# FP4 MLP of a two-layer block: rounding put one pair later, the residual added by TensorE, its result copied by ScalarE

## The reference

```
def fp4_quant_dequant(x):             # blocks of 16 along the last dimension
    scale = maximum(max(abs(xb)) / 6, 1e-12)
    q = GRID[searchsorted(MID, abs(xb / scale))] * sign(xb) * scale
def fp4_linear(x, w):                 # both rounded, then x @ w.T
gate = fp4_linear(x, w_gate)          # 128 -> 352
y = fp4_linear(x, w_up)               # 128 -> 352
h = silu(gate) * y
x = x + tanh(g_ffn[1]) * fp4_linear(h, w_down)     # 352 -> 128
```

## Time and profile before

| | |
|---|---|
| median of 3 runs | 299.23 us (297.94 to 299.8) |
| the profiled execution | 295.81 us |
| its span | 293.8 us |
| mean granted TensorE clock | 0.971 |
| busy: PE / PEld / DVE / ACT / POOL | 89% / 69% / 68% / 55% / 41% |

### The profile page before, as it was taken

The page is one execution under the profiler, slowest core; times in us unless marked ns, Lnnn a source line. Parts: engine busy times, 40 slices in busy tenths (PEclk is TensorE's granted clock), DMA queues, the critical chain, the costliest instruction groups (busy, mean ns, idle before and its releaser), DMA issues.

```text
span 293.8 us, 6298 instructions
## 1 busy us (share of the span) xinstructions
PE 261.2 (89%) x2190; PEld 203.5 (69%) x2190; DVE 199.5 (68%) x538; ACT 161.4 (55%) x368; POOL 120.8 (41%) x172
## 2 busy tenths in 40 slices
PE   8999899999899999999999998987857869696955
PEld 5655466666578789999999975554645547374855
DVE  3997588889987744322222269746287999998981
ACT  2579975555786666666666647224443824443421
POOL 4573879995203042299522015302253131313121
PEclk9999999999999999999999999999998969797999
DMA  7997000000001197767777300000000000000001
GB/s 204 370 363 316 3 2 0 2 2 2 2 3 20 73 379 325 294 287 288 288 289 300 134 0 2 1 3 0 0 0 0 2 1 0 18 19 19 18 19 56
DMA packets 12159, 30.15 MB, mean 103 GB/s; under 512 B 992, under 2 KB 5216, under 8 KB 12000
## 3 DMA queue, kind: packets, MB, share of 16 engines
q1 hardware_dynamic: 12128, 29.75, 26.8%
HBM read 9.75 MB, written 1.05 MB: 37 GB/s over the span
## 4 chain that ended last, share of the span: by engine, by line
PE 63%; DVE 17%; ACT 7%; issue 5%; POOL 3%; DMA 2%; SPq 1%; DVEq 0%; ACTq 0%; POOLq 0%
PE ps L1307 11%; PE ps L1296 11%; PE ps L1156 5%; PE ps L1130 4%; PE ps L1485 4%; PE ps L1143 4%; DVE s_region L279 4%; PE ps L1058 3%; PE ps L1424 3%; PE ps L1049 2%; DVE s_small L228 2%; PE ps L1166 2%; PE ps L1050 2%; DVE s_region L995 2%; DVE s_small L1005 1%
## 5 line engine op out<-in xcount | busy, mean ns | idle before, releaser
L573 ACT ACTIVATE s_region<-ps,s_region 128x128 f32<-128x128 f32 x144 | 41.1, 369 | 22.0 <-PE ps L1296 21.8
L868 DVE SCALAR_TENSOR_TENSOR s_ctxT<-ps,s_region,s_ctxT 128x64 f32 x72 | 18.1, 282 | 44.3 <-PE ps L1307 44.2
L1296 PE MATMUL ps<-s_region 128*128 128x128 f32 x288 | 38.5, 276 | 0.3
L1307 PE MATMUL ps<-s_region 128*128 128x128 f32 x288 | 37.9, 275 | 0.0
L286 POOL TENSOR_TENSOR s_region<-s_region,s_small 128x704 f32<-128x704 f32 (+2 forms) x13 | 17.5, 1343 | 46.5 <-DVE s_region L279 46.5
L1296 PEld LDWEIGHTS ps<-s_region 128*128 128x128 f32 x288 | 35.0, 192 | 1.0 <-DMA s_region<-s_wall 0.6
L1307 PEld LDWEIGHTS ps<-s_region 128*128 128x128 f32 x288 | 35.0, 192 | 0.2 <-issue 0.2
L251 POOL TENSOR_TENSOR s_small<-s_small,s_par 128x4 f32<-128x4 f32 (+3 forms) x14 | 15.5, 1107 | 43.2 <-DVE s_small L234 43.2
L1485 PE MATMUL ps<-s_region 128*128 128x352 f32 x64 | 26.4, 570 | 2.3 <-ACT s_region L650 2.3
L398 POOL COPY s_region<-s_xt 128x64 f32 x72 | 14.8, 238 | 32.1 <-PE ps L1296 22.0
L733 DVE TENSOR_REDUCE s_small<-ps 128x16 f32<-128x1024 f32 x16 | 19.6, 1225 | 9.9 <-PE ps L1130 9.9
(11 more groups left out here) (216 smaller groups left out, 509.0 us busy)
## 6 DMA issues: line engine op xcount, KB each, us to landing
s_region<-s_wall SPq DMA_DIRECT2D x36, 514.0 KB, 3.0
s_wall<-wall SPq DMA_DIRECT2D x8, 514.0 KB, 9.0
s_par<-par SPq DMA_DIRECT2D x1, 1316.0 KB, 10.5
s_x<-x SPq DMA_DIRECT2D x2, 512.0 KB, 6.8
out<-s_x SPq DMA_DIRECT2D x8, 128.0 KB, 1.8
s_region<-ffn SPq DMA_DIRECT2D x1, 560.0 KB, 3.6
s_ctxT<-ctxT SPq DMA_DIRECT2D x2, 256.0 KB, 4.2
s_ctxT<-ctxT SPq DMA_DIRECT2D x1, 512.0 KB, 6.7
```

The source lines that it names most:

```text
L573: ins = act.activation(hg[j % 3][:, c, :], ps[:, j % 3, RPT * S * c:RPT * S * (c + 1)], ACT.Gelu, bias=wbuf[j % 6][:, FF + FC * D + c:FF + ...
L1296: ins = mm(ps[:, j % 3, RPT * S * c:RPT * S * (c + 1)], w[:, P * c:P * c + P], xg[j % 4], start=True, stop=True)
L1307: ins = mm(ps[:, 4 + j % 2, 0:RPT * S], w[:, FF + D * c:FF + D * c + D], hg[j % 3][:, c, :], start=(c == 0), stop=(c == FC - 1))
```

## The change

VectorE's `pair_step(q)` does product, maximum, scale, reciprocal and shrinking of pair q first, and then the rounding of q-1. Its `finish` is gone. The gate is multiplied into the turned w_down by ScalarE as it copies it. In `down(q)` TensorE first multiplies x of the pair (256 columns) with the identity into bank 7 and then adds the six products to it; ScalarE's new `finish(q)` copies the sum back to x. On TensorE down now stands ahead of gate_up in an iteration and works on pair q-3, turn_h on q-2, and turn_x stands ahead of keep_clock. On ScalarE the copy to hT is of pair q-2, behind finish(q-3).

```diff
@@ weights_turned
-                act.copy(dst, ps[:, 2 + g % 2, 0:MT * P]).then_inc(m["wq_used"], 1)
+                src = ps[:, 2 + g % 2, 0:MT * P]
+                ins = act.activation(dst, src, ACT.Identity, scale=tg[:, 3:4]) if g == 2 else act.copy(dst, src)
+                ins.then_inc(m["wq_used"], 1)
@@ scalar
+            def finish(q):
+                act.wait_ge(m["dn_done"], q + 1)
+                act.copy(x[:, 2 * q:2 * q + 2, :].rearrange("p t d -> p (t d)"), ps[:, 7, 0:2 * D]).then_inc(m["x4_done"], 1)
+
+            for q in range(PAIRS + 2):
                 if q + 1 < PAIRS:
                     silu(q + 1)
                 if q < PAIRS:
                     magnitude(q)
                 if q in (1, 3):
                     x_magnitude((q + 3) // 2)
-                if q >= 1:
-                    act.wait_ge(m["ht_done"], q)
-                    act.copy(hT[(q - 1) % 2]...).then_inc(m["ht_used"], 1)
+                if q >= 3:
+                    finish(q - 3)
+                if q >= 2:
+                    act.wait_ge(m["ht_done"], q - 1)
+                    act.copy(hT[q % 2]...).then_inc(m["ht_used"], 1)
                 if q in (0, 2, 4):
                     turned_x(q // 2 + 1)
+            finish(PAIRS - 1)
@@ vector, pair_step(q)
                     dve.tensor_tensor(hh[u], sg[u], ps[:, 3:5, 0:MLP], ALU.mult).then_inc(m["hh_done"], 1)
-                if second:
-                    dve.wait_ge(m["hm_done"], q)
-                    dd.step(fp4_off(dve, hd[w], hm[w], hh[w]...))
-                    fp4_off(dve, hd[w], hm[w], hd[w]).then_inc(m["hd_done"], 1)
...
-                if q >= 3:
-                    finish(q - 3)
...
                     fp4_shrunk(dve, blocks(flat), blocks(flat), spread(hin[n3], 2 * NH)).then_inc(m["hv_done"], 1)
+                if 1 <= q <= PAIRS:
+                    dve.wait_ge(m["hm_done"], q)
+                    if q >= 3:
+                        dve.wait_ge(m["hq_done"], q - 2)
+                    dd.step(fp4_off(dve, hd[w], hm[w], hh[w]...))
+                    fp4_off(dve, hd[w], hm[w], hd[w]).then_inc(m["hd_done"], 1)
@@ tensor
+                mm(ps[:, 7, 0:2 * D], ident, x[:, 2 * q:2 * q + 2, :].rearrange("p t d -> p (t d)"), start=True, stop=False)
...
-            for q in range(PAIRS + 2):
+            for q in range(PAIRS + 3):
+                if q >= 3:
+                    down(q - 3)
                 if q + 1 < PAIRS:
                     gate_up(q + 1)
-                if q >= 2:
-                    down(q - 2)
-                if 1 <= q <= PAIRS:
-                    turn_h(q - 1)
+                if 2 <= q <= PAIRS + 1:
+                    turn_h(q - 2)
+                if q in (0, 2, 4):
+                    turn_x(q // 2 + 1)
                 if q < 2:
                     keep_clock(4, 7)
                 if PAIRS - 2 <= q <= PAIRS:
                     keep_clock(9 if q == PAIRS - 2 else 3, 0)
-                if q in (0, 2, 4):
-                    turn_x(q // 2 + 1)
```

More of the change, by code:

```diff
@@ L678, in _ @@
             normalise(act, 12, 16, m["xn_d"], 14)
-            for q in range(PAIRS + 1):
+            def finish(q):
+                act.wait_ge(m["dn_done"], q + 1)
+                act.copy(x[:, 2 * q:2 * q + 2, :].rearrange("p t d -> p (t d)"), ps[:, 7, 0:2 * D]).then_inc(m["x4_done"], 1)
+            for q in range(PAIRS + 2):
                 if q + 1 < PAIRS:
@@ L685, in _ @@
                     x_magnitude((q + 3) // 2)
-                if q >= 1:
-                    act.wait_ge(m["ht_done"], q)
-                    act.copy(hT[(q - 1) % 2].rearrange("p a k b -> p a (k b)"), ps[:, 5:7, 0:MT * P]).then_inc(m["ht_used"], 1)
+                if q >= 3:
+                    finish(q - 3)
+                if q >= 2:
+                    act.wait_ge(m["ht_done"], q - 1)
+                    act.copy(hT[q % 2].rearrange("p a k b -> p a (k b)"), ps[:, 5:7, 0:MT * P]).then_inc(m["ht_used"], 1)
                 if q in (0, 2, 4):
                     turned_x(q // 2 + 1)
+            finish(PAIRS - 1)
         @block.vector
@@ L990, in pair_step @@
                 u, w, n3 = q % 2, (q - 1) % 2, q % 3
-                first, second = q < PAIRS, 1 <= q <= PAIRS
-                if first:
+                if q < PAIRS:
                     dve.wait_ge(m["sg_done"], q + 1)
@@ L995, in pair_step @@
                     dve.tensor_tensor(hh[u], sg[u], ps[:, 3:5, 0:MLP], ALU.mult).then_inc(m["hh_done"], 1)
-                if second:
-                    dve.wait_ge(m["hm_done"], q)
-                    dd.step(fp4_off(dve, hd[w], hm[w], hh[w].rearrange("p a n -> p (a n)")))
-                    fp4_off(dve, hd[w], hm[w], hd[w]).then_inc(m["hd_done"], 1)
-                if first:
                     if q >= 3:
@@ L1012, in pair_step @@
                     fp4_shrunk(dve, blocks(flat), blocks(flat), spread(hin[n3], 2 * NH)).then_inc(m["hv_done"], 1)
[L1014 to L1017, removed]
+                if 1 <= q <= PAIRS:
+                    dve.wait_ge(m["hm_done"], q)
+                    if q >= 3:
+                        dve.wait_ge(m["hq_done"], q - 2)
+                    dd.step(fp4_off(dve, hd[w], hm[w], hh[w].rearrange("p a n -> p (a n)")))
+                    fp4_off(dve, hd[w], hm[w], hd[w]).then_inc(m["hd_done"], 1)
             def out_and_stats(g):
@@ L1029, in _ @@
             x_scale(1)
-            for q in range(PAIRS + 3):
+            for q in range(PAIRS + 1):
                 pair_step(q)
@@ L1508, in down @@
                         n = min(P, MLP - P * k)
-                        ins = mm(ps[:, 7, D * t:D * t + D], hT[q % 2][0:n, t, k, :], wdT[0:n, k, :], start=(k == 0), stop=(k == MT - 1))
+                        ins = mm(ps[:, 7, D * t:D * t + D], hT[q % 2][0:n, t, k, :], wdT[0:n, k, :],
+                             start=False, stop=(t == 1 and k == MT - 1))
                 ins.then_inc(m["dn_done"], 1)
```

## The result

The kernel after takes 300.32 us (median of 20 runs, 298.88 to 303.65), the kernel before 298.56 (20 runs, 295.34 to 299.94). The ratio is 1.0084, 95% interval 1.0049 to 1.012: slower by 2.5 us, 1.5 to 3.6. The ratio is one of means and leaves out the runs over 1.5% above the fastest of their kernel, so it gives 2.5 us where the medians lie 1.8 us apart. The difference is clear of noise, yet under the 1% that the prediction took as the bound between slower and unchanged. I had said 303.1.

What follows compares the result with a forecast made beforehand. VectorE bounds the kernel before; TensorE, at 5.85 us per pair, was to bound plain steps after. Span 293.8 + 3.9 = 297.7, profiled execution 299.7, and the median's 3.4 shift gave 303.1 us, range 299.8 to 307.

Steps and rivals of the forecast that it cites:

- rival A: The walk's own outcome: TensorE becomes the bound in plain steps; 303.1 us, own range 301.5 to 305, chance 0.43.
- Rival C: Milder: x's roundings don't wait for GpSimd, or the clock stays high over the 5 us gap; 301.1 to 301.9, chance 0.28.
- Part 1: VectorE: plain step 5.06 against 5.43 us; x_scale pays 0.7 and x_round 1.3 each, meeting GpSimd's unscale.
- Part 2: TensorE: copy exposed between turn_h and down, identity product 0.43; 5.85 us per pair, so TensorE bounds plain steps.
- Part 3: ScalarE: gate in the weights costs 0, finish takes 0.45 us, standing ahead of the copy that down(q-2) awaits.
- The walk: Step-by-step timing of the new order from product(1) to the last finish: span ends 3.9 us later, 297.7.
- step 2: TensorE idle 5.1 us before turn_x(2), then slow clock through down(0), 3.9 us; gate_up(4) sets product(4) at 259.85.
- rival B: Clock recovers later, or falls again around turn_x(3), slowing gate_up(5) or gate_up(6) by 1.7 to 2.5; 305 to 307, chance 0.18.
- Rival D: VectorE sets the pace to the end, winning 0.37 in seven steps; -3.0 us, giving 296.2, chance 0.11.

Runs made afterwards that it cites:

- e1: Kernel after with gate_up(q+1) ahead of down(q-3) on TensorE; 1.007 of before, stage 64.66 us.
- e7: Kernel after with x_round and x_scale ahead of the pair's rounding on VectorE, x_unscale ahead of the pair's unscale on GpSimd; 0.9949 of before, stage 59.45 us.
- e11: e7 with keep_clock(3) for keep_clock(9), 10 idle products ahead of turn_x(2), 8 ahead of down(1); 0.9906 of before, median 295.51 us.
- e4: Kernel before with only VectorE's rounding of q-1 moved behind the shrinking of q, finish staying on VectorE; 1.0101 of before, stage 62.88 us.
- e10: Kernel after with 21 idle products ahead of turn_x(2) and 6 ahead of turn_x(3) on TensorE; stage 62.68 us.
- e2: Kernel after with x_round and x_scale ahead of the pair's rounding on VectorE, GpSimd's order unchanged; 1.0109 of before, stage 62.63 us.
- e3: Kernel after with the edits of both e1 and e2; 1.0149 of before, stage 65.35 us.
- e6: Kernel after with keep_clock(3) instead of keep_clock(9) in the iteration of gate_up(7); 1.011 of before, stage 62.53 us.
- e9: Kernel after without the identity product and the gate in the weights, finish back on VectorE; 1.0103 of before, stage 63.21 us.

## Why the prediction was right

Direction and range came out: 300.32 lies just inside 299.8 to 307. The mechanism is that of rival A, but the number is not: A's own range was 301.5 to 305, and 300.32 falls into the 299 to 301 that I had put under C for the case that nothing is seen. The size was too large by 2.8 us, and the side of the 1% bound was the wrong one (I gave slower 0.58, within 0.35).

- **Part 1, VectorE's new order.** Right. Products of a plain step are 5.12 to 5.13 apart where nothing else bounds (e1, e7, e11), for 5.06 in the sum; L1010 is 0.19. x_scale pays 0.69 (0.87 - 0.18), for 0.7. x_round(2) pays 1.07 net (4.21 - 3.14), for 1.3. e4 shows that this part alone is enough for the loss ahead of product(7).
- **Part 2, TensorE's new order.** Right as a bound, 5.95 for 5.85, and the identity product is the 0.43 estimated (255.90 to 256.33 in e10). But e1 shows that covering the copy in the steps wins nothing by itself, since the same work then lies in the tail.
- **Part 3.** Finish 0.37, for 0.45.
- **The walk.** In the first profile, counted from product(0), it gave 12.3 us for product(2), measured 12.34; 28.9 for product(4), measured 27.54; 36.6 for product(5), measured 35.07; 43.0 for product(6), measured 42.90; 49.0 for product(7), measured 48.85; tail 15.6, measured 15.48. The error at product(4) is step 2: I let the slow clock last through all of down(0), 3.9 us, and it took 2.68 with its identity product (257.00 to 259.68). gate_up(4) was done in time, and VectorE set product(4). The agreement at product(6) is luck: the 1.6 us too many at product(5) were met by a fall of the clock at down(2) and gate_up(6) that rival B had and A had not. The repeat fits the walk without it: 28.60 for product(4), which waited for gate_up(4) as the walk has it, then 36.14, 42.32 and 48.26, and a tail of 15.49. In the tail the walk is right for its reason too: four downs are left there, 3.48 to 3.59 us apart (3.5 forecast), where before has three.
- **From the profile to the runs.** This is where the 2.8 us lie. 0.7 of them come from the base: three runs gave 299.23 for before, 20 runs give 298.56. The other 2.1 are the walk's +3.9, which the medians show as 1.8 and the ratio as 2.5. The walk's figure is fair for the stage, which lost 3.1 to 3.7 in the profiles, but the interval of the runs, 1.5 to 3.6, holds the 3.1 and neither 3.7 nor 3.9. Why the runs lose less than the profiled stages is open. Ahead of the stage, product(0) lies at 230.91 to 235.36 in the fourteen profiles, and 1.6 and 1.8 us apart in the two of one kernel; that was in neither sum nor range by name.
- **Rival D** (VectorE sets the pace to the end, 296.2) fell to 5.95 in step 6-7. **Rival C**'s second half came true in part: in the first profile the clock came back sooner. Its first half did not: e2 and e7 show x_round waiting for GpSimd.

The Trainium skill, "SBUF — State Buffer", section "Who interferes with whom", says that which of the two issues first decides who waits, and for the whole instruction. Both directions are in the rows: VectorE's passes longer (4.21 for 3.14) and GpSimd's unscale longer (1.77 for 1.39). The whole instruction is borne out by L269, which ends with the unscale; the passes lost 1.07 us beside an unscale of 1.39.

## What to carry to other kernels

When an instruction is moved on one engine, list the queues of the others that stand behind it: the loss here was not in what VectorE did per step, which fell, but in GpSimd's unscale landing on the scale and the rounding of x, and, behind product(7), in a fourth down with its identity product. That down(0), which is ready, stands behind turn_x(2) on TensorE cost 1.1 us in one profile of after and nothing in the other; no run moves it alone. Put independent work that reads SBUF twice where GpSimd is idle, and move its follow-up on GpSimd in the same edit; e2 without that has a stage 1.1 to 1.7 us shorter than after's, which its runs do not show, e7 with it 4.3 to 4.9 us. And compare stages between fixed marks in two or more profiles of each kernel, when the executions of one kernel differ by more than the change.

## What the runs showed that I had not expected

- Two executions of one kernel put the clock's falls in different places with the same idle times: gate_up(6) behind 1.98 us of idle time 3.19 us, behind 2.04 us 2.53 us. In before the tail took 14.12 or 15.47.
- Filling a gap of 5.62 us with 42 records (4.85 us) of idle products was followed by a clock of 1.0 through the rest of the stage, also over 2.78 us of idle time ahead of down(1), and delayed nothing. In every profile with after's order and no idle products there (after twice, e1, e2, e3, e6, e9) turn_x(2) or what follows it ran at the low clock, except in e7, where the gap was 2.72 us.
- ScalarE copies 128x256 from PSUM in 0.35 to 0.37 us, less than VectorE's 0.48 for the same size with multiply and add; it was the cheapest part of the change.
